# A chain of four attention and feed-forward layers in one kernel: half of the second wide attention's probability tiles are turned by DMA transposes instead of TensorE

## What is computed

```python
# L2 cross attention: 16 heads of 64, 256 queries and 512 keys for each of 2 batches
scores = jnp.einsum('bqhd,bkhd->bhqk', q * SCALE, k)
attn = jax.nn.softmax(scores, axis=-1)
out = jnp.einsum('bhqk,bkhd->bqhd', attn, v).reshape(B, SQ, INNER)
...
# last block (L3_ffn): rows of x are gathered by a router's top k
x_sel = x[bidx, sel_idx]
hn = rmsnorm(x_sel, ln1)
q = rope(heads(hn @ wq), pos_sel)
```

## Time and profile before

| | us |
|---|---|
| median of 3 runs (534.74 to 536.90) | 536.22 |
| the profiled execution, its own time | 535.3 |
| its span, first to last instruction | 533.3 |
| second wide attention, first scores to last values | 358.8 to 464.1 of the span |
| first wide attention, turns on PE | from 28.3 of the span |
| last block, from the last layer norm | 498.9 to the end |

### The profile page before, as it was taken

How to read it: one execution, slowest core, us unless ns; L and a number is a source line. 1 busy time by engine, 2 the same in 40 slices (tenths; PEclk the granted TensorE clock), 3 DMA queues, 4 the chain that set the end, 5 groups by cost and what they waited for, 6 DMA issues and landing times.

```text
span 533.3 us, 13277 instructions
## 1 busy us (share of the span) xinstructions
PE 497.5 (93%) x4894; PEld 289.6 (54%) x4902; DVE 434.2 (81%) x1216; ACT 340.8 (64%) x684; POOL 263.3 (49%) x289
## 2 busy tenths in 40 slices
PE   8889999999999899998899899998999999999996
PEld 3346655556953233334334466835666667954574
DVE  7999999999585888826886799887888888687653
ACT  5688888888437366644565678638888888423112
POOL 7957778887652924410013635135776776300100
PEclk9999999999999999999999999999999999999999
DMA  9751000001040000000002031000000001100000
GB/s 223 144 158 46 1 2 2 2 2 37 7 159 0 1 1 2 2 2 0 1 2 80 2 100 59 2 1 1 2 1 3 1 2 36 47 0 1 2 0 21
DMA packets 24083, 15.42 MB, mean 29 GB/s; under 512 B 8083, under 2 KB 22230, under 8 KB 23894
## 3 DMA queue, kind: packets, MB, share of 16 engines
q1 hardware_dynamic: 24022, 14.60, 10.3%
HBM read 14.33 MB, written 0.26 MB: 27 GB/s over the span
## 4 chain that ended last, share of the span: by engine, by line
PE 55%; DVE 17%; issue 15%; ACT 6%; POOL 4%; DMA 1%; DVEq 0%; SPq 0%; POOLq 0%; ACTq 0%
PE pspair L525 9%; PE psO L540 5%; PE psM L477 5%; PE psS L511 4%; PE psO L750 3%; PE pspair L511 3%; PE pspair L725 3%; ACT PP L1372 3%; PE pspair L1030 3%; DVE nmx L1861 2%; DVE Zt L1748 2%; PE psS L699 1%; PE psS L1002 1%; PE pspair L559 1%; DVE V L1688 1%
## 5 line engine op out<-in xcount | busy, mean ns | idle before, releaser
L525 PE MATMUL pspair<-ident,PP 128*128 128x128 f32 x512 | 82.1, 283 | 2.4 <-ACT PP L1372 2.1
L525 PEld LDWEIGHTS pspair<-ident,PP 128*128 128x128 f32 x512 | 54.2, 141 | 29.7 <-issue 20.9
L540 PE MATMUL psO<-V,PP 128*128 128x64 f16 x1536 | 65.7, 193 | 2.6 <-DVE Oall L1795 2.0
L540 PEld LDWEIGHTS psO<-V,PP 128*128 128x128 f16 x1536 | 60.0, 98 | 7.8 <-DVE PP L1755 2.9
L1438 ACT ACTIVATE PP<-pspair 128x1024 f32<-128x1024 f32 x48 | 46.5, 1021 | 24.2 <-PE pspair L736 24.0
L1755 DVE TENSOR_TENSOR PP<-pspair,PP 128x512 f16<-128x512 f32 x66 | 45.4, 687 | 18.8 <-ACT PP L1356 18.7
L2455 POOL TENSOR_TENSOR ln_rs<-ln_ve,minus_half 128x4 f32<-128x4 f32 x10 | 10.3, 1032 | 80.8 <-DVE ln_ve L1645 77.7
L1372 ACT ACTIVATE PP<-scores_m,nm 128x512 f32<-128x512 f32 x64 | 46.5, 727 | 5.4 <-DVE nm L1739 5.4
L2466 POOL TENSOR_TENSOR PP<-acc,one 128x512 f16<-128x512 f32 x32 | 33.3, 1039 | 32.9 <-ACT acc L1354 32.8
L2466 POOL TENSOR_TENSOR PP<-y_sb,one 128x512 f16<-128x512 f32 x30 | 31.2, 1040 | 21.2 <-ACT y_sb L1354 21.2
L1356 ACT CAST PP<-pspair 128x512 f16<-128x512 f32 x66 | 38.3, 580 | 0.9 <-PE pspair L525 0.9
(11 more groups left out here) (604 smaller groups left out, 1243.8 us busy)
## 6 DMA issues: line engine op xcount, KB each, us to landing
W<-in_L_ffn_W SPq DMA_DIRECT2D x16, 256.0 KB, 2.9
bigw<-in_L_xattn_w_q SPq DMA_DIRECT2D x2, 512.0 KB, 6.9
bigw<-in_L_xattn_w_kv SPq DMA_DIRECT2D x1, 1024.0 KB, 4.8
V<-in_ctx SPq DMA_DIRECT2D x1, 512.0 KB, 4.7
bigw<-in_L_xattn_w_v SPq DMA_DIRECT2D x1, 512.0 KB, 5.9
mask_b<-in_mask_BxS_ff SPq DMA_DIRECT2D x1, 512.0 KB, 7.7
bigw<-in_L_xattn_w_k SPq DMA_DIRECT2D x1, 512.0 KB, 6.1
bigw<-in_L_xattn_w_o SPq DMA_DIRECT2D x1, 512.0 KB, 3.8
```

Of the source, the lines that this page charges most:

```text
L525: mm = pe.transpose(bank[f"T{j % 2}"][:, k * P:(k + 1) * P], Pb[j % 4][:, k * P:(k + 1) * P], ident[:])
L540: mm = pe.matmul(bank["O"][:, (j % UPH) * a.dv:(j % UPH + 1) * a.dv], (PTH, PTL)[ppart][j % 4][:, k * P:(k + 1) * P], (VH, VL)[vpart][:, b ...
```

## The change

In the second wide attention (L2X) alone, `own_low` is turned round. Odd units (and unit 0) go the old way over PE, with ACT's cast and DVE's subtraction. The 31 even units from 2 to 62 no longer go through PE, a T bank or ACT's copy. POOL halves the unturned tile: `split_unturned` reads `Pb` and writes both halves side by side (128 x 1024 f16) into `acc` or `y_sb`, which it may do once the DMA of two even units before has landed. SP then issues one DMA transpose of the eight 128 x 128 blocks into the unit's `PTH` and `PTL`, once POOL is done and the `values` of four units before have been made. `values` is four rounds behind instead of three, and stands ahead of `turn` in the round. DVE's `norm` moves behind `stat` and `recip` in its round. SP's loads for later stages stand behind the last transpose.

In the last block the two gathers (L1142, L1148) are done with f16 halves: ACT writes the high half of XN, POOL the low half and the halves of `xw`; ACT widens the f16 `pick` for the later f32 matmuls. The router's weight is gathered by itself (`wsel`), in f32, later, in the place of three spares. The remaining edits to POOL give its waits on itself one semaphore (`link`) in the place of several, with the same instructions.

```diff
+BY_DMA = ("L2x",)
...
-        self.lag = 3
+        self.by_dma = name in BY_DMA
+        self.lag = 4 if self.by_dma else 3
...
+        self.turns = self.units // 2 + 1 if self.by_dma else self.units
...
+        PS = [t.bitcast(F16) for t in P32]
+        PTD = [t[:].bitcast(F16).rearrange("p (c q) -> p c q", q=P) for t in PT]
...
+        XN16 = W1[0][:].bitcast(F16).rearrange("p (h t d) -> p h t d", h=2, t=NT)
+        xw16 = W1[1][:].bitcast(F16)[:, 0:NT * 2 * (NXW - 1)].rearrange("p (t h c) -> p t h c", t=NT, h=2)
...
         def own_low(a, i, j):
...
+            if a.by_dma:
+                return j % 2 == 1 or i * UPI + j == 0
             return not j % 2 or i * UPI + j == a.units - 1
...
+        def turn_bank(a, i, j):
+            k = i * UPI + j
+            if a.by_dma:
+                k = (k + 1) // 2
+            return f"T{k % 2}", k // 2
+        def nth_own(a, i, j):
+            k = i * UPI + j
+            return (k + 1) // 2 + 1 if a.by_dma else k // 2 + 1 + k % 2
+        def nth_dma(i, j):
+            return (i * UPI + j) // 2 - 1
...
-                reuse(f"{n}.T{j % 2}", affine(i, j, UPI, 2))
+                b, nth = turn_bank(a, i, j)
+                reuse(f"{n}.{b}", nth)
                 for k in range(a.kt):
-                    mm = pe.transpose(bank[f"T{j % 2}"][:, k * P:(k + 1) * P], Pb[j % 4][:, k * P:(k + 1) * P],
-                                      ident[:])
-                mm.then_inc(full[f"T{j % 2}"], 1)
+                    mm = pe.transpose(bank[b][:, k * P:(k + 1) * P], Pb[j % 4][:, k * P:(k + 1) * P], ident[:])
+                mm.then_inc(full[b], 1)
...
-                if not own_low(a, i, j):
+                if own_low(a, i, j):
+                    b, nth = turn_bank(a, i, j)
+                    emptied(pe, f"{n}.{b}", nth)
+                elif a.by_dma:
+                    dma_done(pe, a, nth_dma(i, j))
+                else:
                     pe.wait_ge(sem(f"{n}.split"), affine(i, j, UPI, 2) + 1)
...
+                elif a.by_dma and j % 2 == 0:
+                    mm.then_inc(sem(f"{n}.pv"), 1)
...
                     if j % 2 and not (last and j + AHEAD >= UPI):
                         pair_scores(*shift(i, j + AHEAD))
-                    turn(i, j)
-                    if not (first and j < a.lag):
+                    if a.by_dma and not (first and j < a.lag):
+                        values(*shift(i, j - a.lag))
+                    if own_low(a, i, j) or not a.by_dma:
+                        turn(i, j)
+                    if not a.by_dma and not (first and j < a.lag):
                         values(*shift(i, j - a.lag))
...
+            pe.wait_ge(sem("L3f.xlow"), 1)
             for b in range(B):
                 pe.wait_ge(sem("L3f.pick"), b + 1)
-                for k in range(2):
-                    mm = pe.matmul(ps[:, b * SLOTS:(b + 1) * SLOTS], XN[0][:, 2 * b + k, :],
-                                   pick[:, 2 * b + k, 0, b * SLOTS:(b + 1) * SLOTS], start=(k == 0), stop=(k == 1))
+                for m in range(4):
+                    k, h = divmod(m, 2)
+                    mm = pe.matmul(ps[:, b * SLOTS:(b + 1) * SLOTS], XN16[:, h, 2 * b + k, :],
+                                   pick16[:, 2 * b + k, 0, b * SLOTS:(b + 1) * SLOTS], start=(m == 0), stop=(m == 3))
             mm.then_inc(full["O"], 1)
-            pe.wait_ge(sem("L3f.xw"), 2)
             ps = take(pe, "L3f.xs", "S3")
             for t in range(NT):
-                mm = pe.matmul(ps[:, 0:NXW], pick[:, t, :, :].rearrange("p r s -> p (r s)"), xw[:, t, :],
-                               start=(t == 0), stop=(t == NT - 1))
+                mm = pe.matmul(ps[:, 0:2 * (NXW - 1)], pick16[:, t, :, :].rearrange("p r s -> p (r s)"),
+                               xw16[:, t, :, :].rearrange("p h c -> p (h c)"), start=(t == 0), stop=(t == NT - 1))
             mm.then_inc(full["S3"], 1)
+            spare(pe, "T0", 1)
...
-                    spare(pe, "T0", 3)
+                    pe.wait_ge(sem("L3f.xw"), 1)
+                    ps = take(pe, "L3f.wsel", "S3")
+                    for t in range(NT):
+                        mm = pe.matmul(ps[:, 0:1], pick[:, t, :, :].rearrange("p r s -> p (r s)"), xw[:, t, 0:1],
+                                       start=(t == 0), stop=(t == NT - 1))
+                    mm.then_inc(full["S3"], 1)
...
+                if a.by_dma and not own_low(a, i, j):
+                    return
...
+                    if a.by_dma and not own_low(a, *before_):
+                        act.wait_ge(sem(f"{n}.split"), nth_dma(*before_) + 1)
+                    else:
+                        b, nth = turn_bank(a, *before_)
+                        filled(act, f"{n}.{b}", nth)
...
+            act.wait_ge(sem("L3f.xn"), NT)
+            nc.scalar.copy(XN16[:, 0, :, :], XN[0][:]).then_inc(sem("L3f.xhigh"), 1)
             act_copy(act, "L3f.xt", XT[0][:])
+            act.wait_ge(sem("L3f.pick"), B)
+            nc.scalar.copy(pick[:], pick16[:]).then_inc(sem("L3f.picked"), 1)
...
+                if g == 0:
+                    ps = filled(act, "L3f.wsel")
+                    nc.scalar.copy(xs[:, 0:1], ps[:, 0:1]).then_inc(free_of("L3f.wsel"), 1)
...
-                        if j % 4 == 3 and not (first and j < UPH):
+                        if j % 4 == 3 and not (first and j < UPH) and not a.by_dma:
                             norm(*group)
...
+                        if j % 4 == 3 and not (first and j < UPH) and a.by_dma:
+                            norm(*group)
                         if own_low(a, i, j):
                             evac(i, j)
...
-                dve.tensor_copy(xs[:], ps[:, 0:NXW]).then_inc(free_of("L3f.xs"), 1)
+                dve.tensor_reduce(xs[:, 1:NXW], ps[:, 0:2 * (NXW - 1)].rearrange("p (h c) -> p c h", h=2), AX.X, ALU.add)\
+                    .then_inc(free_of("L3f.xs"), 1)
...
+            def link(ins):
+                chain[0] += 1
+                ins.then_inc(sem("pool_chain"), 1)
+                pool.wait_ge(sem("pool_chain"), chain[0])
...
+                def split_unturned(i, j):
+                    d = nth_dma(i, j)
+                    if a.mask:
+                        pool.wait_ge(sem(f"{n}.exp"), i * UPI + j + 1)
+                    else:
+                        emptied(pool, f"{n}.S{j % 4}", affine(i, j, UPI, 4))
+                    if d >= 2:
+                        dma_done(pool, a, d - 2)
+                    high = PS[d % 2][:, 0:SK]
+                    link(pool.tensor_tensor(high, Pb[j % 4], one[:].broadcast_to([P, SK]), ALU.mult))
+                    pool.tensor_tensor(PS[d % 2][:, SK:2 * SK], Pb[j % 4], high, ALU.subtract)\
+                        .then_inc(sem(f"{n}.split"), 1)
                 def rounds(i, first, last):
-                    for j in range(1, UPI, 2):
+                    for j in range(UPI):
                         if not own_low(a, i, j):
-                            split(i, j)
+                            (split_unturned if a.by_dma else split)(i, j)
...
+            link(pool.tensor_copy(xw16[:, :, 0, :], xw[:, :, 1:NXW]))
+            link(pool.tensor_tensor(xw16[:, :, 1, :], xw[:, :, 1:NXW], xw16[:, :, 0, :], ALU.subtract))
+            pool.wait_ge(sem("L3f.xhigh"), 1)
+            pool.tensor_tensor(XN16[:, 1, :, :], XN[0][:], XN16[:, 0, :, :], ALU.subtract).then_inc(sem("L3f.xlow"), 1)
...
+            def sp_turn(a, i, j, meanwhile=None):
+                d = nth_dma(i, j)
+                sp.wait_ge(sem(f"{a.name}.split"), d + 1)
+                if i * UPI + j >= 4:
+                    sp.wait_ge(sem(f"{a.name}.pv"), (i * UPI + j - 4) // 2 + 1)
+                sp.dma_start_transpose(out=PTD[j % 4], in_=PS[d % 2]).then_inc(sem(f"{a.name}.turned{d % 2}"), 16)
+            def sp_attention(a):
+                def rounds(i, first, last):
+                    for j in range(0, UPI, 2):
+                        if not own_low(a, i, j):
+                            sp_turn(a, i, j)
...
+            sp_attention(L2X)
             filled(sp, "L2x.proj", L2X.per * (NPAIR - 1) - 1)
```

79 lines of the change are left out of this document (36 added, 43 removed).

## The result

The changed kernel takes **548.8 us** (median of 4 runs, 547.75 to 549.0) against 535.6 us for the kernel before in the same comparison (4 runs, 534.74 to 536.9). The ratio is 1.0238 [1.0222, 1.0253]: 2.4% slower. It was forecast at 529.3 us, inside a range of 522.5 to 549.0. The profiled execution took 548.81 us, with a span of 547.1.

A forecast was written before the change was run, and what follows sets the result against it. PE was taken as nearly full, with the loop through POOL and DMA to set the pace after the change; terms summing to -6.85 us gave 528.4 for the profiled execution, 529.3 as median, range 522.5 to 549.

The forecast's parts named there:

- 10.05 if the hold goes as well: PE in the second wide attention: work per eight units falls from 12.37 to 10.49 us, or 10.05 without the 0.44 hold.
- 6.5 eights x (12.37 - 11.5): -5.65: Second wide attention: 6.5 periods of eight units shrink from 12.37 to 11.5 us each, saving 5.65 us.
- 10.66 us stay: DVE in the second wide attention: still subtracts 33 units, so its 10.66 us per eight units remain.
- the loop of POOL and DMA: Second wide attention: POOL's halving and the transpose's landing set the pace, 11.16 us for eight units.
- L: Time for a DMA transpose to land in the second wide attention: taken as 3.1 us, break-even at 3.7.
- The last eight units: End of the second wide attention, without projections: four turns fewer, half of at most 1.9 us taken, -0.9 us.
- the drain: End of the second wide attention: unit 62's late transpose, mostly filled by PE's output sums, costs +0.3 us.
- The last block: Gathers with f16 halves let the projection start at 509.4 in place of 510.05: -0.6 us.
- SP's later loads: Loads for later stages move behind the last transpose, by some 8 us, at a cost of 0.
- Rival 1: Second wide attention: transposes land late, L of 3.9 to 5, giving 549 us at 4.6 or 545 at 4.3; 15%.
- Rival 3: Second wide attention: bank O's hold at its upper end, or L of 3.6, eats the gain: 535 us; 18%.
- Rival 2: Second wide attention: a tile's blocks transpose one after another, landing several times a copy's: 589 us; 9%.

The follow-up runs named there:

- e14: e12 with a third buffer between POOL and the transposes: 531.24 us.
- e11: Changed kernel with DVE's subtraction of the odd unit one round later, behind the next pair's first maximum: 538.18 us.
- e12: e9 with DVE's subtraction of the odd unit one round later, as in e11: 531.73 us.
- e13: e11 with two sum banks used in turn: 538.30 us.
- e7: e4 with groups of four units summed alternately in banks O and T1, all turns in T0: 532.64 us.
- e10: e7 with a third buffer between POOL and the transposes: 533.30 us.
- e3: Changed kernel with a third buffer for the halves that the DMA transposes read: 549.23 us.
- e4: Changed kernel with the parity turned, odd units 1 to 61 by POOL and DMA, even ones and 63 over PE: 536.28 us.
- e8: Changed kernel with groups of four units summed alternately in banks O and T1, all own turns in T0: 549.26 us.
- e6: Changed kernel with both values of two rounds on the even round and DVE's query low half before the odd unit's subtraction: 543.89 us.
- e9: e6 with the two sum banks of e7: 540.56 us.

## Why the prediction was wrong

**What bounds the kernel: half right.** PE was full, as the earlier trace rows show. But the period of 12.37 was read as PE's work plus a hold of 0.44 us, and the hold as slack that may go with the turn. It was the one visible place of loop 1: scores, turn, cast, exp, scores, 2.86 us. PE's three other passes (3.16 us) hid it. That loop does not get shorter when PE has less to do, so "10.05 if the hold goes as well" was never on offer, and with passes of at least 2.86 us four times in eight units neither was 10.49. With the odd unit's turn behind the scores 11.44 is the floor (e14), and 6.5 x (12.37 - 11.44) = 6.0 us all that this stage could give up to its last eight units.

**DVE's order: the step that failed.** The term that came out wrong is the first of the sum, "6.5 eights x (12.37 - 11.5): -5.65": with a period of 14.10 it is +11.2. The prediction said of DVE that only odd units are subtracted in place of even ones, so its 10.66 us stay. The sum did stay (10.95 in the row above). The place did not: the subtraction went from behind the next maximum to ahead of it, and so into the path of the exp. That is loop 2, 3.2 us, and through bank M the projection's 1.35 us. Moving that instruction alone gives 10.6 of the 13.2 us back (e11): of the 2.60 us between the forecast period and the measured one, 1.31 go with it. Another 1.06 go from e11 to e12, with the values off the odd rounds (the query's half and the banks moved too, but the banks give nothing on e11: e13); 0.23 stay.

**PE's order: shown, and not priced.** The order rows ahead of the prediction show values between scores and turn on the odd round. They add 0.34 us to loop 1 (3.20 in place of 2.86), four times in eight units: 1.36 us, and 6.5 x 1.36 = 8.8 us that the sum does not have. e11, held by loop 1 alone, has that period: 12.79, against 11.44 + 1.36 = 12.80. From e11 to e12 6.5 us of them come back; there the loop of POOL and DMA stops the gain.

**The loop through POOL and DMA: its sizes right, its role wrong.** L was taken as 3.1 and is 3.0 in the median. (The prediction says that the sixteen loads it was taken from had nothing else in the queue; some were issued 0.4 us behind another, at 290.22 and 290.66 of the kernel before.) POOL's two operations end 2.27 us after their start. The loop takes 5.49 us where 5.58 was forecast. The chain that ended last runs through it only in versions in which the other loops have been shortened: e12 with a period of 11.7 and 531.7 us, e7 with 532.6. Those two come within 3.5 us of the forecast's 529.3, but in neither is it the only limit: a third buffer gives 0.5 us on e12 (e14) and nothing on e7 (e10). In the changed kernel a third buffer for this loop gives nothing (e3).

**The other terms.** The last eight units were to give 0.9 us and the drain to cost 0.3. From the first scores to the last ones the stage got 13.4 us longer (93.0 to 106.4), of which 6.5 x 1.73 = 11.2 are the period; the run-in, the last eight units and the drain behind the last scores (16.3 to 18.1) cost the other 4 us. Near the end (463.96, 468.30 and 472.11) PE waits three times for DVE's `bigw` (L1736), 1.0 to 1.2 us each; no run took that apart. The last block was right: -0.7 for a forecast of -0.6. Its rows, against the earlier trace rows:

```profile
523.05 0.36 PE L1184 MATMUL psO<-pick,W 128*128 128x32 f16 x8
523.26 0.25 PE L1189 MATMUL pspair<-W,pick 128*128 128x18 f16 x4
...
523.84 0.62 PE L1196 MATMUL psS<-l3w,hnT 128*64 128x256 f32 x2
```

From the first gather to the projection are 0.79 us where they were 1.78. SP's later loads cost nothing that shows, as forecast.

**The rivals.** None of the three is what happened. Rival 1 gave 545 to 549 us for a late landing, and 548.8 was measured; that agreement is luck, since half of the landings took 3.0 us, the longest 4.7, and POOL waited for none of them from 365 to 450. It is also why the range holds the time, just. Rival 3 had the sum bank as the holder: true of e4, where two banks give 3.6 us (e7), and not of the changed kernel (e8). The chance of 58% for faster rested on adding up engines and one loop. A rival that follows each value through all engines that work in order, with the subtraction's new place in it, was missing.

**The pages.** That X-bar transposes are as fast as regular copies (the Trainium skill, Advanced Engine Details and Errata, section X-Bar Transpose (TRN2)) agrees with this case: 3.0 us for a transposed tile of 256 KB, 3.0 for a plain load of 256 KB in the same run. The prediction's "by that L would be 2.9 and DVE the bound" was a slip: its loop is then 2 x 5.38 = 10.76 us, still 0.1 above DVE's 10.66. The 1309 ns of the Trainium skill, VectorE: DVE Perf Modes, section The three transpose paths, do not add up over the blocks of one DMA: eight blocks would need 10.5 us, the prediction's estimate, and landed in 3.0. Rival 2 falls with it.

## What to carry to other kernels

When work is taken from the full engine, first list the loops that go through several in-order engines (here scores, turn, cast, exp, and cast, subtraction, maximum, exp), add up each one's length for as many units as it covers, and take the longest, not the largest engine sum: as long as a turn stands right behind the scores, 11.44 us was the floor before anything was changed. An unexplained short wait of the full engine is the place where such a loop shows. When a step changes its round, look on every engine at what it now stands ahead of; and a single removal that gives nothing clears nothing: two sum banks give 0 on the changed kernel (e8), 3.6 us on e4 (e7), and 3.3 from e6 to e9.

## What the runs showed of the hardware

- A DMA transpose of 128 x 1024 f16 costs SP 1.23 us to issue in most cases, and lands 3.0 us after its start at the least. Each adds 1056 packets: the page counts 56819 in place of 24083, 32736 more for 31 transposes, and 32736 of those are under 512 B (40819 in place of 8083). The DMA engines are still only half busy (share 0.48 at a period of 14.1 us; in e14 0.50 and 0.58 in two stretches of 11.48).
- Two transposes close behind each other do not both land in 3.0 us. In e12 the second of two issued 2.23 us apart took 4.66 us; with 3.8 us or more between them the chain shows 3.04, with 3.25 anything from 3.04 to 4.20. SP in time, and the chain's row of the same transpose:

```profile
391.08 1.23 SPq L2767 DMA_TRANSPOSE PP<-acc  x1
393.31 1.23 SPq L2767 DMA_TRANSPOSE PP<-y_sb  x1
```

```profile
393.31 4.66 DMA PP<-y_sb
```

Landings of up to 4.9 us were seen in e14, and of up to 5.5 in e10. So the loop through the DMA is longer than its shortest round whenever POOL catches up, and in e12's chain such rounds lie between the short ones (y_sb is issued at 393.31 and again at 400.40, 7.09 us later). Why the second lands late was not tested.
- DVE and POOL are not slowed by landing transposes: the subtraction takes 0.69 us (0.68 in the earlier trace rows), POOL's pair 2.27 us (2.27 in the earlier trace rows, which the prediction rounded to 2.28).
